# Epsilon and negation as operations of two tensors, one subtraction put between scatters, and one set of moments put behind another, in a gated scan and top-1 mixture-of-experts kernel

## The reference

```
u = layernorm(x)
g = sigmoid(u @ Wg.T + bg);  h = scan of h[t] = (1 - g[t]) * h[t-1] + g[t] * u[t]
x = x + layernorm(h @ Wo.T + bo)
v = layernorm(x)
e = argmax(softmax(v @ router_w + router_b))          # 8 experts
rank = how many earlier tokens chose the same expert;  valid = rank < 320
y = valid:      relu(v @ w1[e] + b1[e]) @ w2[e] + b2[e]
    otherwise:  relu(v @ ow1 + ob1) @ ow2 + ob2       # overflow layers, hidden size 1024
out = x + layernorm(y)
```

## Time and profile before

| | |
|---|---|
| median of 3 runs | 1178.93 us (1178.27 to 1179.01) |
| the profiled execution, its own time | 1179.15 us |
| its span in the trace | 1177.3 us |
| PE, DVE, ACT, POOL busy | 1131.3, 1044.9, 767.5, 647.7 us |
| granted PE clock | 0.998 of full |

### The profile page before, as it was taken

The page is one execution under the profiler, slowest core; times in us unless marked ns, Lnnn a source line. Parts: engine busy times, 40 slices in busy tenths (PEclk is TensorE's granted clock), DMA queues, the critical chain, the costliest instruction groups (busy, mean ns, idle before and its releaser), DMA issues.

```text
span 1177.3 us, 24621 instructions
## 1 busy us (share of the span) xinstructions
PE 1131.3 (96%) x7341; PEld 991.5 (84%) x7341; DVE 1044.9 (89%) x2793; ACT 767.5 (65%) x1433; POOL 647.7 (55%) x734
## 2 busy tenths in 40 slices
PE   8999999999999999999999999999999999999996
PEld 4788888888888888888888888888888888899996
DVE  6888899999999999999999999999999988778885
ACT  4366666666667666666666666766766667678783
POOL 3556656665555655555666555565555555414544
PEclk9999999999999999999999999999999999999999
DMA  8211132222222222222222222222222130245440
GB/s 252 65 45 63 33 107 78 68 66 55 71 71 71 71 71 68 66 68 58 61 65 60 54 71 71 71 71 71 69 66 68 50 104 19 80 146 181 147 132 34
DMA packets 186314, 92.46 MB, mean 79 GB/s; under 512 B 121403, under 2 KB 182509, under 8 KB 186148
## 3 DMA queue, kind: packets, MB, share of 16 engines
q1 hardware_dynamic: 179108, 86.65, 26.5%
q0 software_dynamic: 7168, 5.34, 1.5%
HBM read 53.82 MB, written 38.76 MB: 79 GB/s over the span
## 4 chain that ended last, share of the span: by engine, by line
DVE 46%; PE 32%; issue 16%; ACT 2%; POOL 2%; DVEq 1%; DMA 0%; ACTq 0%; POOLq 0%
DVE st L940 11%; DVE hid_lo L1104 5%; PE psY L1528 5%; PE psY L1531 4%; PE psY L1530 4%; PE psH L1420 4%; PE psH L1421 4%; PE psH L1422 4%; DVE mv L947 3%; DVE psT L983 3%; DVE ysb L1118 3%; DVE outt L1034 2%; DVE att L1011 2%; DVE xfT_lo L1048 2%; DVE hst L1005 2%
## 5 line engine op out<-in xcount | busy, mean ns | idle before, releaser
L1528 PE MATMUL psY<-W_hi,hid_hi 128*128 128x256 f32 x1168 | 339.6, 291 | 27.2 <-DVE hid_lo L1104 27.1
L1531 PE MATMUL psY<-W_hi,hid_lo 128*128 128x256 f32 x1168 | 330.2, 283 | 0.0
L1530 PE MATMUL psY<-W_lo,hid_hi 128*128 128x256 f32 x1168 | 330.0, 283 | 0.0
L686 ACT ACTIVATE hid<-psH,biasT 128x512 f32<-128x512 f32 (+1 forms) x312 | 201.7, 647 | 154.9 <-PE psH L1422 153.4
L1528 PEld LDWEIGHTS psY<-W_hi,hid_hi 128*128 128x128 f32 x1168 | 222.4, 190 | 52.3 <-DVE hid_lo L1104 39.6
L453 POOL TENSOR_TENSOR rstd<-veps,mhalf 128x4 f32<-128x4 f32 (+2 forms) x103 | 124.1, 1205 | 203.9 <-DVE nmean L952 203.9
L1420 PE MATMUL psH<-xfT_hi,W_hi 128*128 128x512 f32 (+1 forms) x624 | 235.9, 378 | 0.3 <-ACT hid L686 0.2
L1421 PE MATMUL psH<-xfT_lo,W_hi 128*128 128x512 f32 (+1 forms) x624 | 234.9, 376 | 0.0
L1422 PE MATMUL psH<-xfT_hi,W_lo 128*128 128x512 f32 (+1 forms) x624 | 232.7, 373 | 0.0
L1530 PEld LDWEIGHTS psY<-W_lo,hid_hi 128*128 128x128 f32 x1168 | 222.9, 191 | 3.4
L1531 PEld LDWEIGHTS psY<-W_hi,hid_lo 128*128 128x128 f32 x1168 | 222.8, 191 | 0.0
(11 more groups left out here) (177 smaller groups left out, 2213.8 us busy)
## 6 DMA issues: line engine op xcount, KB each, us to landing
xin<-L_attn_x SPq DMA_DIRECT2D x32, 512.0 KB, 3.5
stage<-L_ffn_w SPq DMA_DIRECT2D x16, 1024.0 KB, 5.7
out<-outt SPq DMA_DIRECT2D x31, 512.0 KB, 2.8
stage<-L_attn_x SPq DMA_DIRECT2D x26, 512.0 KB, 3.4
stage<-tok SPq DMA_DIRECT2D x416, 32.0 KB
xbuf<-zrow SPq DMA_DIRECT2D x1, 2590.0 KB, 17.1
xin<-xbuf SPq DMA_DIRECT2D x8, 259.0 KB, 5.2
stage<-L_ffn_ow SPq DMA_DIRECT2D x2, 1024.0 KB, 9.2
```

The source lines that it names most:

```text
L686: act.activation(hid[j % 2][:, at:n], psH[:, j % 2, at:n], ACT.Relu, bias=bias).then_inc(s_hid, 1)
L1528: pe.matmul(dst, hi, w[0][:, j, :], start=(j == 0 and (tail or t % 2 == 0)), stop=False, skip_group_check=True)
L1530: pe.matmul(dst, hi, w[1][:, j, :], start=False, stop=False, skip_group_check=True)
L1531: last = pe.matmul(dst, lo_, w[0][:, j, :], start=False, stop=(j == HC - 1), skip_group_check=True)
```

## The change

There are three edits. First, `veps` and `nmean` are made by `tensor_tensor` with small constant tensors (`eps_t`, `minus`, set once by two memsets) where they were `tensor_scalar` with an immediate number; a semaphore for the memsets is waited for. Second, in the general step of POOL, `state_lo` stands between the second and the third scatter, where it stood behind the fourth. Third, in the general step of DVE, set 0's `bn_stats` stay where they were, but its `bn_aggr`, `veps` and `nmean` come behind those of set 3.

```diff
+        eps_t = sb("eps_t", [P, TG])
+        minus = sb("minus", [P, TG])
...
+            dve.memset(eps_t[:], EPS)
+            dve.memset(minus[:], -1.0).then_inc(s_eps, 1)
...
                 dve.wait_ge(s_ag[k], cnt(g, 1, 1) + base)
-                dve.tensor_scalar(veps[k][:, t0:n].unsqueeze(2), mv[k][:, t0:n, 1:2], EPS, None, ALU.add)
-                dve.tensor_scalar(nmean[k][:, t0:n].unsqueeze(2), mv[k][:, t0:n, 0:1], -1.0, None, ALU.mult)\
+                dve.wait_ge(s_eps, 1)
+                dve.tensor_tensor(veps[k][:, t0:n].unsqueeze(2), mv[k][:, t0:n, 1:2], eps_t[:, t0:n].unsqueeze(2), ALU.add)
+                dve.tensor_tensor(nmean[k][:, t0:n].unsqueeze(2), mv[k][:, t0:n, 0:1], minus[:, t0:n].unsqueeze(2), ALU.mult)\
                     .then_inc(s_ve[k], 1)
...
                 if live(now, NG):
-                    dispatch(now, range(TG))
+                    dispatch(now, range(0, 2))
                 if live(far, NG):
                     state_lo(far)
+                if live(now, NG):
+                    dispatch(now, range(2, TG))
...
                 if live(next_x, NG):
-                    stats0(next_x)
+                    read_rows0(next_x)
                 if run and not up:
                     xf_lo((0, 0), C, NG)
                 if run:
                     result(now, ob2_b[:].unsqueeze(1), TG, t0=sure(now))
                 if run and up:
                     stats3(now, TG, t0=sure(now))
+                if live(next_x, NG):
+                    moments(0, next_x, TG)
```

More of the change, by code:

```diff
@@ L258, in sandwich_kernel @@
         s_seen = sem("s_seen")
+        s_eps = sem("s_eps")
         s_scat = sems("s_scat")
```

## The result

The changed kernel takes 1139.45 us (median of 4 runs, 1139.44 to 1139.56), against 1178.92 us (4 runs): a ratio of 0.9667, with a 95% interval of 0.965 to 0.9683. It is 39.5 us faster. The forecast was 1143 us, with a range of 1138 to 1160.

A forecast was written before the change was run, and what follows sets the result against it. PE was taken as the bound, held up by DVE's late hid_lo because hst_lo held veps 2.47 us a step; 36 us off 1179.15 gave 1143.1, adjusted by 0.2 to 1143 us, range 1138 to 1160.

The forecast's parts named there:

- the ceiling: On PE over the whole kernel: no edit on another engine can give more than PE's about 46 us of idle time.
- the long step's other 0.49 us: In PE's 32.18 us step, beyond the 1.31 us lost before layer 2: 0.49 us of smaller waits for hid_lo and att.
- its low end: For tensor_tensor veps and nmean with nothing else changed: 0 gained as low end, 25 x 2.47 us of DVE time as high.
- 0.7 us for `hid_lo` 3: On DVE before PE's layer 2 of block 3: hid_lo would end about 0.7 us before PE wants it.
- 36 us: Whole gain over 25 steps: 12.5 pairs at 2.94 us give 36.8 us, taken as 36.
- PE's own length of a step: PE's step in the loop without its waits: 30.38 us, from the short step's 31.52 less 1.14.
- the first and the last step: Of the 25 steps, these two were taken as shorter by some tenths, so 36.8 us became 36.
- The hold did not move: Rival: POOL's tok holds choose's last two-input operations on DVE, up to 0.55 us each; up to 1167 us, chance 0.13.
- No chain through POOL and ACT: Rival: POOL's powers of sets 1 and 2, ACT and DVE's x1 end last; about 1161 us, chance 0.10.
- The changed kernel does what it says: Rival denied here: scatters hold the two-input form as hst_lo held the old one; 1177 to 1181 us, chance 0.04.
- The slower case: Rival: POOL holds the new form in all four sets, for most of a scatter or power; 1214 us, chance 0.05.
- All signs: Expected profile: veps at most 0.2 us, hst_lo between scatters, transposes 30.4 us apart, little hid_lo wait, DVE waiting before result.

The follow-up runs named there:

- The form alone: The kernel before with only veps and nmean changed to tensor_tensor with constant tensors, both orders as before: 1178.23 us, ratio 0.9992.
- the two orders alone: Two runs, the kernel before with only state_lo between the scatters, or only set 0's bn_aggr, veps and nmean behind set 3's: 1140.16 us and 1139.57 us.

## Why the prediction was right

**The bound.** PE held up by `hid_lo` of block 3, and `hid_lo` late because `veps` was held under `hst_lo`: this stands. In each of 25 steps `veps` took 2.57 to 2.79 us and ended 0.03 or 0.04 us behind the second `hst_lo`. (The 61.8 us of the group hold two short holds outside these steps as well, 0.59 us at 28.80 and 0.46 us at 122.66.) The form alone leaves 83.9 us in the group and 1178.2 us. Each of the two orders alone takes the hold away, or all but 0.2 us of it, and 39 us with it.

What does not stand is the ceiling: that PE's 46 us of idle time are the most that an edit on another engine can give. The span became 39.8 us shorter, but only 27.4 us of that were idle time of PE (46.0 before, 18.6 after); the other 12.4 us had been booked as busy. Matmul rows overlap when they follow each other closely, and around a wait they do not, so that part of what a wait costs is covered by longer busy time: 1.31 us by the starts of the earlier trace rows are 1.15 in the brackets, and of the long step's other 0.49 us the rows of PE show 0.11 as idle. The ceiling was not reached here, so the forecast did not suffer.

**The edits' shares.** Counting 0 for the form was right, and its low end was the true one. For the two orders, the working had each of them clear `veps`, but never said that one would be enough; that the third gives nothing on top of the second, or the other way round, only the experiments show. It also placed `bn_stats` and `result` beside the subtractions and expected no hold there, and there was none.

**The spare time.** 0.7 us for `hid_lo` 3 was foretold, and 0.71 us measured in the tighter step. It was missed that the other step has 0.99.

**The sum.** 36 us were forecast and 39.5 measured. The term that was mis-sized is PE's own length of a step, 30.38 us. From 149.26 to 906.33 the changed kernel has 25 steps, 757.07 us, so 30.28 each; before, the same 25 took from 149.82 to 946.03, 796.21 us. That is 39.1 us. With 30.38 they would give 796.21 - 759.5 = 36.7. The 0.10 us a step, 2.5 us in all, is a second price of a wait, which I had not taken off: in the kernel before, the matmul behind the one that waited starts 0.22 us after it and not 0.12 (timeline of PE, before). That the 0.49 us of the long step were waits too was right, for both kinds of step are now equal.

```profile
586.09 0.28 PE L1530 MATMUL psY<-W_lo,hid_hi 128*128 128x256 f32 x1
```

The one that waited is that of 585.87 in the earlier trace rows. In the changed kernel the two start at 533.13 and 533.25. The rest is that I rounded the first and the last step down by 0.8 us, which was not called for, and that the step before the 25, where PE had lost 0.4 us to a wait as well, became 0.55 us shorter.

**The rivals.** The hold did not move: `choose` does overlap `tok` now, and `cand` at 553.51 still takes 0.19 us. No chain through POOL and ACT took PE's wait over. The changed kernel does what it says. The slower case would have needed holds under scatters and powers, and the new form takes 0.16 us in all 26 places where `veps` starts inside a power, and wherever it starts inside a scatter.

**What was to be seen.** All signs came but two. `veps` is not 0.2 us at most everywhere: 0.60 us at 28.76, beside POOL's `W_lo`, and 0.31 us at 93.93, beside `hst_lo`, are still held, though together they are worth no more than 0.6 us of DVE's time. And DVE does not wait for PE before `result`. It starts `ysb` at 546.88, 0.08 us behind `bn_stats`, since DVE and PE reach that point together.

## What to carry to other kernels

A 128x4 operation that takes 2.6 us is not computing, and DVE's busy time hides it: compare the longest of a group with its median, and lay the long ones beside POOL's timeline. If they end with a wide POOL operation, move either of the two; here moving one was enough, and a second input tensor instead of an immediate changed nothing. And before the gain is counted, find how long the fed engine's step is without its waits. Count a wait of PE by the starts of its matmuls, and not by the idle time in the view of waits: here one cost 0.16 us more than was shown as idle, and 0.10 us more for the matmul behind it. PE's idle time in the page was no ceiling for that reason.

## What the runs showed of the hardware that I had not expected

- A VectorE operation of 128x4 is held for 2.46 us by POOL's 128x512 subtraction whether it has one SBUF input (2.64 us) or two (2.62 us), and over both of POOL's back-to-back instructions. In 13 of the 25 holds of the kernel before, the record of `veps` starts first, by 0.03 to 0.18 us, and `veps` is still the one that waits. The Trainium skill names two kinds of VectorE operation that fall under one lock (SBUF — State Buffer, section "SBUF: two separate sides"): one that runs in a perf mode with two ports, and one with two SBUF inputs beside a GpSimd operation that reads SBUF. The run with the form alone agrees for the second; whether the one-input form ran in such a mode no run shows.
- POOL's power on 128x4, which also reads SBUF, runs for 1.04 us and holds neither form (0.17 and 0.16 us inside it). By the same rule of the Trainium skill a two-input operation would be blocked for the whole instruction; here the measurement says otherwise. Whether POOL takes the ports only for the short time in which it reads 4 elements was not tried.
- POOL's `tok` holds `cand` in some places and not in others. In the changed kernel `cand` takes 0.43 and 0.50 us beside `tok<-xin` (both times that they meet, ahead of the 25 steps, as in the earlier trace rows), and 0.19 to 0.23 us beside `tok<-stage` (13 times, as at 553.51). The operations are the same and the tile that POOL reads is another; why this matters was not tried.
